# Output products of one attention kernel spread over the next group's heads, with turned rows issued by ScalarE

## What is computed

```python
def _L1_cond_ref(x, Wq, Wk, Wv, Wo, ..., k_cache, v_cache, block_table, cache_seqlens):
    q = jnp.einsum('bsd,ed->bse', x, Wq).reshape(bsz, seqlen, HQ, D)
    k = ...; v = ...
    q = _rope(_rmsnorm(q, q_norm_w), pos); k = _rope(_rmsnorm(k, k_norm_w), pos)
    kc = k_cache[block_table].reshape(bsz, L, HK, D)      # 512 cached keys
    k_all = jnp.concatenate([kc, k], axis=1)              # and 32 new ones
    ...
    scores = jnp.einsum('bqhd,bkhd->bhqk', q, k_all) * SCALE
    scores = jnp.where(valid[:, None, None, :], scores, -1e+30)
    probs = jax.nn.softmax(scores, axis=-1)
    o = jnp.einsum('bhqk,bkhd->bqhd', probs, v_all)
    o = o.reshape(bsz, seqlen, HQ * D)
    return jnp.einsum('bse,de->bsd', o, Wo)
x = x + _L0_cond_ref(x, itok_B_0_30, L0_cond_weights)
x = x + _L1_cond_ref(x, ...)
```

## Time and profile before

| | us |
|---|---|
| median of 3 runs | 1043.12 |
| lowest and highest | 1042.54, 1044.98 |
| the profiled execution | 1038.51 |
| its span, from its first to its last instruction | 1036.7 |

### The profile page before, as it was taken

The page is one execution under the profiler, slowest core; times in us unless marked ns, Lnnn a source line. Parts: engine busy times, 40 slices in busy tenths (PEclk is TensorE's granted clock), DMA queues, the critical chain, the costliest instruction groups (busy, mean ns, idle before and its releaser), DMA issues.

```text
span 1036.7 us, 24928 instructions
## 1 busy us (share of the span) xinstructions
PE 977.4 (94%) x8329; PEld 775.4 (75%) x8329; DVE 795.4 (77%) x1706; ACT 713.1 (69%) x1943; POOL 495.6 (48%) x642
## 2 busy tenths in 40 slices
PE   3889999999889999899999999999999999999998
PEld 2678888887678788668868857866976986895793
DVE  6789999999997788757857866865875884785680
ACT  4788999988765788647846755764864774675670
POOL 6455666566881266526424623632540641552340
PEclk9999999999999999999999999999999999999999
DMA  5789999989989899768998998997999999899840
GB/s 201 252 303 337 320 384 369 384 279 399 377 289 319 313 329 356 263 186 271 344 252 260 339 266 218 330 299 203 343 295 229 308 317 240 258 359 252 239 147 11
DMA packets 268017, 296.49 MB, mean 286 GB/s; under 512 B 94065, under 2 KB 225649, under 8 KB 265329
## 3 DMA queue, kind: packets, MB, share of 16 engines
q1 hardware_dynamic: 249200, 227.65, 71.7%
q0 software_dynamic: 18688, 67.25, 18.7%
HBM read 231.77 MB, written 46.27 MB: 268 GB/s over the span
## 4 chain that ended last, share of the span: by engine, by line
PE 56%; DVE 14%; SPq 8%; DMA 6%; issue 6%; ACT 6%; POOL 3%; ACTq 0%; DVEq 0%; POOLq 0%
PE ps_o L1410 16%; PE ps_proj L1410 16%; PE ps_o L1488 8%; SPq L641 5%; PE ps_s L1448 4%; PE ps_s L1452 4%; PE ps_t L1459 3%; DMA kt<-k_pages_t 3%; DVE probs L1150 2%; PE ps_rt L1558 2%; DMA vs<-v_pages,v_row 2%; DVE c_stage L1306 1%; PE ps_o L1502 1%; DVE rot L1278 1%; DVE pt L1170 1%
## 5 line engine op out<-in xcount | busy, mean ns | idle before, releaser
L868 POOL TENSOR_SCALAR probs<-probs,recip 128x544 f32<-128x544 f32 (+1 forms) x256 | 158.4, 619 | 376.9 <-DVE recip L1158 373.0
L933 ACT ACTIVATE probs<-probs,neg_max 128x544 f32<-128x544 f32 x256 | 191.3, 747 | 158.2 <-DVE neg_max L1150 157.5
L1150 DVE CUSTOM_DVE_ANT_0 probs<-ps_s,mask,row_scale 128x544 f32<-128x544 f32 x256 | 200.1, 782 | 121.2 <-PE ps_s L1452 118.7
L1488 PE MATMUL ps_o<-pt,vs 128*128 128x128 f16 x3072 | 213.0, 219 | 5.4 <-DVE result L1192 2.5
L1488 PEld LDWEIGHTS ps_o<-pt,vs 128*128 128x128 f16 x3072 | 191.1, 98 | 16.3 <-issue 6.6
L822 POOL TENSOR_TENSOR roped<-rot 128x256 f32<-128x256 f32 x160 | 143.8, 921 | 79.4 <-DVE rot L1270 76.9
L1410 PE MATMUL ps_proj<-wt_hi,x0t_hi 128*128 128x512 f32 x384 | 158.6, 413 | 8.7 <-DVE x0t_lo L1108 7.2
L1410 PE MATMUL ps_o<-wo,ot_hi 128*128 128x512 f16 x512 | 153.5, 382 | 10.0 <-DVE ot_lo L1182 10.0
L1410 PE MATMUL ps_proj<-wt_hi,x0t_lo 128*128 128x512 f32 x384 | 150.7, 392 | 0.0
L1410 PE MATMUL ps_proj<-wt_lo,x0t_hi 128*128 128x512 f32 x384 | 149.8, 390 | 0.0
L856 POOL DMA_INDIRECT vs<-v_pages,v_row x128 | 131.7, 1029 | 22.2 <-issue 19.7
(11 more groups left out here) (145 smaller groups left out, 1590.2 us busy)
## 6 DMA issues: line engine op xcount, KB each, us to landing
kt<-k_pages_t SPq DMA_DIRECT2D x512, 128.0 KB
c_nat<-in_L_cond_k_cache SPq DMA_DIRECT2D x32, 512.0 KB, 5.8
q_t<-stage SPq DMA_DIRECT2D x64, 256.0 KB, 7.5
c_nat<-in_L_cond_v_cache SPq DMA_DIRECT2D x32, 512.0 KB, 7.0
qt<-q_t SPq DMA_DIRECT2D x32, 512.0 KB, 5.6
w_nat<-in_L_cond_Wq SPq DMA_DIRECT2D x8, 1024.0 KB, 8.4
k_pages_t<-c_stage SPq DMA_DIRECT2D x16, 512.0 KB, 5.6
c_nat<-in_L_cond_Wo SPq DMA_DIRECT2D x16, 512.0 KB, 8.1
```

The lines of the kernel that those rows point to most:

```text
L868: pool.tensor_scalar(part, part, col(recip, i), 1.0, ALU.mult, ALU.mult).then_inc(p_norm, 1)
L933: act.activation(pr, pr, ACT.Exp, bias=col(neg_max, i), scale=-1.0, accum_out=col(row_sum, i)).then_inc(a_exp, 1)
L1150: dve.tensor_tensor_reduce(out=probs_of(i), in0=ps_s[:, score_cols(i):score_cols(i) + KEYS], in1=mask[(i // HK) % 2][:, mask_at(i):mask_at ...
L1488: ins = pe.matmul(ps_o[n % 2][:, jl * P:(jl + 1) * P], v[:, part, :], pt[i % NPT][:, NCH * half + c, :], start=jl == 0 and c == 0 and k == ...
```

## The change

All of it is in phase two. In the order of the loop:

- **Output products.** They get a PSUM bank of their own, `ps_y`, and `project_out(g, n)` now does one output head (three matmuls). One stands at the end of each step from the last step of the group to step 28 of the next, two at steps 3 and 4 (`Y_AT`). The last group's go in four lots of 4, 6, 6 and 16 behind the last heads (`Y_LAST`). One `add_residual` a group is left, at step 29 of the next group. The bank comes from the transposes, which have three banks up to head 23 and two from then on.
- **Layout of the context.** So that a context can be written while output heads of the last group are still to be read, even groups keep `ot_hi` and `ot_lo` with the output head innermost, odd groups in four blocks with 8 output heads innermost. The stationary operand of an output product is then read with a step of 32 elements (64 bytes) or 8 elements (16 bytes), where its 128 columns lay side by side before. ACT and DVE read `ps_o` with a step of 32 or 64 elements and write runs of 16 or 8. In odd groups tokens stand in another order, which the residual's load and the output's store undo.
- **Turned rows.** From head 24 on each fourth head (27, 31, ..., 255: 58 in place of 64) is turned by DMA. The rows have a tile of their own, two deep, and ACT issues the DMA, as the first thing of step i - 1 of ACT for head i (SP did it in its step i - 2).
- **New keys and values.** `ptn` and `vn` go from 128 to 96 partitions: high values twice, low values once, against the high, low and high part of the probabilities. `weigh_new` has 4 matmuls in place of 8. The high part of `ptn` is written by two ACT instructions of 32 partitions in place of one of 64, the low one by two of DVE, and POOL copies the high part to the third block of partitions (`tn_copy`), which `weigh_new` waits for and which stands ahead of `norm(i + 2)` on POOL. `tn_hi` and `tn_lo` come one step earlier. The two clearings of `vn` at the start are gone.
- **Output weights** are converted in one step of three, steps 1, 4, ..., 58.
- **SP** issues a sequence's queries, all 16 key pages and new values in one go, two sequences ahead.

```diff
-    ptn = [sb(f"ptn{i}", [4 * SEQ, 2, P], F16) for i in range(2)]
-    ot_hi = sb("ot_hi", [P, HQ, GB, SEQ], F16)
+    ptn = [sb(f"ptn{i}", [3 * SEQ, 2, 2, P], F16) for i in range(2)]
+    ot_hi = sb("ot_hi", [P, HQ * GB * SEQ], F16)
+    STAGED = 2
+    rows = sb("rows", [P, STAGED, 2, L], F16)
-    NTB = 3
+    NTB = 2
+    ps_y = psum("ps_y", [P, HID])
...
-    TN, TNE, OE = HPC - 1, HPC, HPC + 2
-    DMA_FIRST, DMA_LAST, STAGED = 2, 11, 3
+    TN, TNE, TNC, OE = HPC - 1, HPC - 1, HPC, HPC + 2
+    DMA_FIRST, T_THIRD = 24, 24
     def by_dma(i):
-        return 0 < i < NP2 and g >= 1 and (DMA_FIRST if g > 1 else 8) <= r <= DMA_LAST
+        return DMA_FIRST <= i < NP2 and i % HPC == HPC - 1
...
+    Y_AT = {r: (r + 1,) for r in range(-1, 3)} | {3: (4, 5), 4: (6, 7)} | {r: (r + 3,) for r in range(5, HQ - 3)}
+    Y_LAST = {-1: range(0, 4), 0: range(4, 10), 1: range(10, 16), 2: range(16, HQ)}
+    def head_tokens(tile, g, n):
+        if g % 2 == 0:
+            return tile[:].rearrange("p (m h) -> p m h", h=HQ)[:, :, n]
+        k, j = divmod(n, QUARTER)
+        return tile[:].rearrange("p (k m j) -> p k m j", k=GB, j=QUARTER)[:, k, :, j]
...
     def late_head(i):
+        k, r = divmod(i, 3)
+        return WO_EARLY + k if i >= 0 and r == 1 and WO_EARLY + k < HQ else None
...
+            def tn_copy(n, normed):
+                pool.wait_ge(a_tnhi, n + 1)
+                pool.wait_ge(p_norm, normed)
+                pool.tensor_copy(ptn[n % 2][2 * SEQ:3 * SEQ], ptn[n % 2][0:SEQ]).then_inc(p_tncopy, 1)
...
+            def turn_rows(i):
+                act.wait_ge(v_plo, dma_no(i + 1))
+                act.wait_ge(t_pv, i - NPT + 1)
+                act.dma_start_transpose(pt[i % NPT][:], rows[:, dma_no(i) % STAGED].rearrange("p s f -> p (s f)")
+                                        ).then_inc(d_pt[i % NPT], 16)
...
-                for m in range(2):
-                    for e in range(2):
-                        v = vn[b % 2][:, 2 * h + m, e]
-                        for part in range(2):
-                            ins = pe.matmul(ps_o[n % 2][:, jl * P:(jl + 1) * P], v[:, part * D:(part + 1) * D],
+                pe.wait_ge(p_tncopy, n + 1)
+                for jl in range(HPC):
+                    ins = pe.matmul(ps_o[n % 2][:, jl * P:(jl + 1) * P], vn[b % 2][:, HPC * h + jl, :],
...
-            def project_out(g, k):
+            def project_out(g, n):
+                if n == 0:
+                    if g == 0:
+                        evacuated(pe, max(m for m in range(len(tjobs)) if t_banks[m] == NTB))
+                    else:
+                        pe.wait_ge(v_res, g)
+                    pe.wait_ge(v_otlo, NBG * (g + 1) - 1)
+                if n == HQ // NHALF:
+                    pe.wait_ge(v_otlo, NBG * (g + 1))
+                hi, lo = head_tokens(ot_hi, g, n), head_tokens(ot_lo, g, n)
+                ins = products(ps_y[:], [(hi, wo[:, h, 0, :]), (hi, wo[:, h, 1, :]), (lo, wo[:, h, 0, :])],
...
-                if y_part(i) is not None:
-                    project_out(*y_part(i))
+                for n in y_heads(i):
+                    project_out(y_group(i), n)
```

More of the change, by code:

```diff
@@ L117, in build @@
     key_pos = sb("key_pos", [P, MASK_W])
-    vn = [sb(f"vn{i}", [4 * SEQ, HK // 2, 2, 2 * D], F16) for i in range(2)]
+    vn = [sb(f"vn{i}", [3 * SEQ, HK, D], F16) for i in range(2)]
     phase1 = ExitStack()
@@ L455, in split_rows @@
     def split_rows(i, part):
-        return wo[:, HQ + dma_no(i) % STAGED, part, :]
+        return rows[:, dma_no(i) % STAGED, part, :]
     def old_keys(i):
@@ L954, in tn_hi @@
                     act.wait_ge(t_pvn, n - 1)
-                act.activation(ptn[n % 2][0:2 * SEQ].rearrange("p m r -> p (m r)"),
-                               ps_t[tjob_no["tn", n] % NTB][0:2 * SEQ, 0:2 * P], ACT.Copy, scale=P_SCALE
-                               ).then_inc(a_tnhi, 1)
+                for e in range(2):
+                    ins = act.activation(ptn[n % 2][0:SEQ, e], turned_new(n, e), ACT.Copy, scale=P_SCALE)
+                ins.then_inc(a_tnhi, 1)
             def ot_hi_of(n):
@@ L1394, in _ @@
                     row_recip(i + 2)
-                if at(i, OE) is not None and y_part(i) is None:
+                if at(i, OE) is not None:
                     ot_lo_of(at(i, OE))
```

198 lines of the change are left out of this document (92 added, 106 removed).

## The result

The changed kernel takes **1207.28 us** (median of 4 runs, 1200.44 to 1216.68), the kernel before 1044.05 beside it. The ratio is 1.156, its 95% interval 1.146 to 1.165. The forecast was 1016, with a range up to 1040. The profiled execution took 1200.44, its span is 1198.7.

What follows compares the result with a forecast made beforehand. PE was taken as the bound, at 95% of what it can stream. Savings of 16.8 + 5.5 + 3 + 1.4 = 26.7 us from 1038.5 gave 1011.8; plus 4.6 for the runs' median, 1016 us, range 1004 to 1040.

Steps and rivals of the forecast that it cites:

- second group: Second group: eight heads turned by DMA here too, moved weight conversions fit on ACT and DVE: -5.5 us.
- five more: Later groups (2 to 7): 80.7 us each instead of 83.5, 2.8 less a group, 16.8 over six.
- the waits that I left in: Groups 2 to 7: 1.0 us of PE waits and 1.1 us of small holes would remain in each.
- last group and end: Last group 2.8 us less; at the end, output heads behind the last heads cover a PE hole, -1.4 us.
- The first group: First group: fewer conversions and new-value matmuls, partly taken back by doubled new-key instructions: -3 us, between 0 and -5.
- The term for the new values: New values on PE: four matmuls fewer for every four heads, -1.8 us a group.
- What is put on ACT: Turned-row DMAs on ACT: issues and landing stay hidden at the median issue of 1.25 us; no cost.
- The third (DMA engines bound, 0.08): Transfers: DMA engines can't give more, groups stay at 83.5 us, total 1033; chance 0.08.
- The second (ACT bound): ACT: issues of 2 to 3 us make ACT the bound and PE wait; 1031, at worst 1045; chance 0.14.
- The fourth (two banks): Transposes: with two PSUM banks PE stops at each head for DVE, 0.2 us each, total 1062; chance 0.07.
- The first (stepped loads): Output products: stepped stationary loads outlast the 216 ns stream; at 300 ns the total is 1081; chance 0.11.
- ACT as issuer: Turned-row DMAs: another issuer saves sequencer time only, since DMAs of several engines share the same 16 DMA engines; little gain.

Runs made afterwards that it cites:

- e11: Changed kernel with all key pages but without the loads of cached values for sequences 2 to 31: 1011.2 us.
- e10: Kernel before without the loads of key pages and cached values for sequences 2 to 31: 1035.2 us.
- e9: Changed kernel without the loads of key pages and cached values for sequences 2 to 31: 1012.5 us.
- e12: Kernel before with only the change's new keys and new values part (96 partitions, four matmuls instead of eight): 1051.7 us.
- e17: Changed kernel with SP issuing turns two steps ahead, its key pages behind them, and GpSimd asking for two value chunks a step from the second group: 1058.9 us.
- e15: Changed kernel with the heads i % 4 == 0 turned by DMA in place of i % 4 == 3: 1085.8 us.
- e8: Kernel before with only the context laid out with the output head innermost, for all groups: 1041.2 us.
- e2: Changed kernel with SP's page loop and waits of the kernel before, but ACT issuing the transposing DMAs: 1168.7 us.
- e1: Changed kernel with SP's loop of the kernel before: SP issues the transposing DMAs two steps ahead, pages meant in fours: 1068.8 us.

## Why the prediction was wrong

- **What the engines can do** was forecast nearly, by terms that miss in both directions. e11 against the profile of before, by groups of 32 heads from one row maximum to the next: second group 86.7 to 80.3, -6.4 (forecast -5.5); five more from 83.0 to 83.7 to 79.0, -22.2 (forecast -2.8 each, -14.0: the waits that I left in, 1.0 and 1.1 a group, went too); last group and end 113.1 to 112.0, -1.1 (forecast, with its share of a group, over 4). The first group gained nothing, 69.9 to 70.9, where -3 was forecast: the doubled instructions took back all that the later conversions gave. With 0.5 us lost ahead of the attention, -28.2 in place of -26.7, close by luck in part. And e11 has no cached values to wait for, while the kernel before gains 9.2 us itself when both loads are left out (e10): like against like, e9 to e10, the change is worth 22.7. The term for the new values (-1.8 a group) came out as a loss in the kernel before (e12) and was never seen by itself in the new one.
- **The step that failed** is in "What is put on ACT": "Landing was 4.2 us, 8.3 at most, and PE takes the rows three steps after the issue, 7.5 us and more: hidden, and the longest just not." The 4.2 and 8.3 were measured where turns went through SP's own queue, between four pages and four pages. The change puts them in another queue, and every second one into 16 pages and the gathers: 13.7 in the median, 16.6 at most. The row was taken over to a place in which its conditions no longer held, and at the same time the cover went from three steps of 4 us to three of 2.5. The cover itself was read rightly: "7.5 us and more" measured 8.3 in the median. The landing was not. The term was 0; it measured 137.4 us of waits.
- **A second term was missing**: the clock. PE's busy time is 1014.2 us, 964.2 in e11, for the same 8097 instructions: 50 us. The granted clock falls to 0.50 at 22 of the 28 waits, not at six of the shorter ones (0.6 to 2.2 us), and is full again 2.9 to 6.1 us after the wait; summed over the time that PE is busy in the attention, what the granted clock lacks comes to 49.7 us. 137.4 + 50.0 is 187.4 of the 190.2 us between the two spans.
- **The rivals.** The third (DMA engines bound, 0.08) named the right engines and a harmless price, 1033: it took for its worst case that a group stays at 83.5. e17's 84 to 90 a group is about that, though its waits are those of one head that is issued late, so it doesn't show a bound; the change itself shows what happens when lateness stops PE, which then stops what frees the buffers. "The share counts waiting packets" was said against it, and the share stands at 0.97 with 262 GB/s in e17 and with 282 before: it does not say what is left. The second (ACT bound) did not come: issues of 1.25 us, ACT busy for 56.5 and with eight issues for 66.5, in the forecast's 65 to 70. The fourth (two banks) is real, 59.4 us in e15, and was avoided here by the choice of heads alone. The first (stepped loads) is out: 145 to 149 ns per load, still under 216. The page that speaks of lines of 16 bytes (the Trainium skill, SBUF — State Buffer, Door 1: The DMA port swizzle) would have it slower; half again as long per load agrees with it, the kernel's time (e8) does not show it.
- **ACT as issuer** was called an issue's place and nothing more, on the rule that DMAs of several issuers run on the same engines and interleave (the Trainium skill, DMA: Bandwidth & Descriptors, Issuing engines are not separate DMA queues). They do interleave (three queues moved packets in the 9 us above), and e2 against e1 shows that the choice of queue can cost more than sequencer time: 100 us.
- **Confirmed by their rows**: no wait for the residual, 0.3 us for `ot_lo` in five groups; four matmuls on new values from 850.97 to 851.19, 0.22 us; products at 0.22 from start to start.

To see in the kernel before, when one knows where to look: how little else moves beside a turned head. Two stretches of 2 us with a turn in them and the one between, and then two without any turn near (same columns):

```profile
706.00:708.00 2.00, 2.00 (x21) 1.40 (x20) 1.45 (x3) 0.67 (x2) 0.00 (x0) 1.00 1.03 157
708.00:710.00 2.00, 2.00 (x13) 1.00 (x11) 0.32 (x2) 1.17 (x4) 0.29 (x1) 1.00 0.91 241
710.00:712.00 2.00, 2.00 (x22) 1.42 (x20) 1.47 (x4) 0.71 (x2) 0.00 (x0) 1.00 0.66 154
...
744.00:746.00 2.00, 2.00 (x26) 1.88 (x25) 2.00 (x8) 1.32 (x3) 0.85 (x2) 1.00 1.00 360
746.00:748.00 2.00, 2.00 (x27) 1.86 (x25) 1.62 (x8) 1.69 (x5) 0.72 (x1) 1.00 1.05 408
```

The kernel before had its turned heads where few other loads were due, and moved 360 to 408 GB/s elsewhere. Part of the low rate is just that: from 710 to 712 the engines' share is 0.66, so they were not all at work; from 706 to 708, at 1.03, they were. The change spreads the turned heads over all steps.

**Open**: why the engines move 169 instead of 377 GB/s while turned rows are among pages and values, and whether the 4 KB packets are the reason; and whether e17 with the turn of 8b+3 ahead of the pages would beat the kernel before. No version of the change with all loads was faster than the kernel before; the 1011 us of e11 were not reached with the cached values in.

## What to carry to other kernels

A landing time belongs to a queue, a moment and a pace: before taking it over, write down what else is queued when the moved DMA is issued, and how many microseconds its cover lasts after the change, since a faster loop shortens the cover of everything in it. Where DMA engines show a share near 1, take a load away in an experiment first: it tells in one run what the engines could do (1011 us here) and what the transfers take back. Look in the trace whether an edit did what its name says: the "fours" of e1 and e2 were 16 pages in a row. And price a stall on PE with the clock that it loses behind it, here a third more.

## What was not expected of the hardware

- A transposing DMA of 0.26 MB lands in 2.7 us in SP's queue with few loads about (the median of e10), and in 13.7 in ACT's queue beside pages and gathers; while one of these was on its way, all queues together moved 169 GB/s, where it had been 377.
- Its issue takes 1.25 us on ACT as on SP.
- In a wait of PE of 6.28 us the granted clock falls to 0.50 and stays there for some 4 us behind it; 22 of 28 waits cost 50 us of PE's time that way.
- A stationary operand of 128 f16 columns with a step of 64 or 16 bytes loads in 145 to 149 ns, side by side in 98. PSUM read with a step of 32 elements costs ACT nothing, 582 ns against 583 (e8).
